# One accumulator and hand-on matmuls in both expert stages, and an up product with the tokens stationary

## What is computed

```python
x = x + 0.5 * ffn(layernorm(x));  x = x + attention(layernorm(x));  x = x + 0.5 * ffn(layernorm(x))

# ffn: E = 64 experts, each token picks K = 6, an expert takes its first CAP = 128 tokens
scores = softmax(xf @ gate_w.T);  _, idx = top_k(scores + gate_b, K)
h  = silu(einsum("ecd,eid->eci", xb, w1)) * einsum("ecd,eid->eci", xb, w3)   # I = 176 hidden
yb = einsum("eci,edi->ecd", h, w2)
y  = zeros_like(xf).at[tok].add(contrib * weight)    # a token can get rows from several experts
z  = silu(xf @ ws1.T) * (xf @ ws3.T) @ ws2.T         # the shared expert, for all tokens
```

## Time and profile before

| | |
|---|---|
| median of three runs | 2036.9 us (2029.87 to 2038.8) |
| the profiled execution | 2036.17 us, its span 2034.4 us |
| PE busy | 1796.7 us (88%) |
| DVE busy | 1274.6 us (63%) |
| ACT busy | 1071.4 us (53%) |
| POOL busy | 873.6 us (43%) |
| granted PE clock, mean | 0.957 of full |

### The profile page before, as it was taken

How to read it: one execution, slowest core, us unless ns; L and a number is a source line. 1 busy time by engine, 2 the same in 40 slices (tenths; PEclk the granted TensorE clock), 3 DMA queues, 4 the chain that set the end, 5 groups by cost and what they waited for, 6 DMA issues and landing times. The chain is left out here.

```text
span 2034.4 us, 33948 instructions
## 1 busy us (share of the span) xinstructions
PE 1796.7 (88%) x11458; PEld 1157.8 (57%) x11458; DVE 1274.6 (63%) x3131; ACT 1071.4 (53%) x2132; POOL 873.6 (43%) x938
## 2 busy tenths in 40 slices
PE   5999997999926799999999999999699999888886
PEld 2566564888813344445545445454356656678786
DVE  4778786444336577777777777773477878744333
ACT  3777664111114577777777777777377766401110
POOL 1011010688736666556655566640101101146675
PEclk9999999999967899999999999999799999989998
DMA  2435442999843344444444444331232433269886
GB/s 86 132 100 164 133 130 103 245 260 260 208 110 94 104 116 116 116 118 125 125 124 119 132 119 116 95 85 43 77 101 79 134 109 103 75 163 227 224 219 120
DMA packets 218389, 270.03 MB, mean 133 GB/s; under 512 B 18394, under 2 KB 185466, under 8 KB 218238
## 3 DMA queue, kind: packets, MB, share of 16 engines
q1 hardware_dynamic: 193662, 230.33, 37.4%
q0 software_dynamic: 24576, 37.77, 9.9%
HBM read 136.17 MB, written 80.38 MB: 106 GB/s over the span
## 5 line engine op out<-in xcount | busy, mean ns | idle before, releaser
L1340 DVE TENSOR_REDUCE a_smax<-a_p_ring 128x1 f32<-128x512 f32 (+2 forms) x768 | 353.8, 505 | 153.7 <-PE a_p_ring L1427 148.6
L1242 ACT ACTIVATE a_probs<-a_p_ring 128x512 f32<-128x512 f32 x640 | 363.9, 606 | 104.2 <-PE a_p_ring L1439 102.6
L1427 PE MATMUL a_p_ring<-p_ks,p_qs 100*128 100x512 bf16 (+3 forms) x1024 | 247.4, 306 | 46.0 <-ACT a_probs L1242 20.6
L634 ACT ACTIVATE e_silu<-e_p_up 88x256 f32<-88x256 f32 x128 | 48.7, 380 | 424.6 <-PE e_p_up L703 328.9
L47 POOL TENSOR_TENSOR f_rstd<-f_mv,eps 128x4 f32<-128x4 f32 x32 | 25.6, 800 | 557.1 <-DVE f_mv L41 552.6
L703 PE MATMUL e_p_up<-e_xT,h_w 128*88 128x128 f32 x2048 | 255.5, 280 | 0.8 <-DVE e_xT L644 0.8
L1439 PE MATMUL a_p_ring<-p_qs,p_ks 103*128 103x512 bf16 (+3 forms) x1024 | 244.2, 305 | 7.0 <-ACT a_probs L1242 6.7
L703 PEld LDWEIGHTS e_p_up<-e_xT,h_w 128*88 128x88 f32 x2048 | 240.4, 163 | 1.3 <-issue 1.1
L455 PE MATMUL f_p_up<-f_xnT,f_ws1T 128*128 128x512 f32 x384 | 188.0, 612 | 1.5 <-ACT f_xnT L250 1.5
L586 POOL DMA_INDIRECT e_got<-rows,slot_token x128 | 127.3, 995 | 140.5 <-issue 134.0
L496 PE MATMUL f_p_z<-f_ws2T,f_hidden 128*128 128x256 f32 (+1 forms) x768 | 184.6, 391 | 1.9 <-DVE f_hidden L343 1.9
(11 more groups left out here) (154 smaller groups left out, 3297.6 us busy)
## 6 DMA issues: line engine op xcount, KB each, us to landing
h_w<-w_in SPq DMA_DIRECT2D x128, 352.0 KB
p_qs<-a_parts SPq DMA_DIRECT2D x192, 128.0 KB, 2.5
p_ks<-a_parts SPq DMA_DIRECT2D x192, 128.0 KB, 2.5
h_w<-w_in SPq DMA_DIRECT2D x128, 176.0 KB
rows<-f_row SPq DMA_DIRECT2D x32, 640.0 KB, 6.8
h_x<-x_in SPq DMA_DIRECT2D x16, 512.0 KB, 5.9
acc<-h_x SPq DMA_DIRECT2D x16, 512.0 KB, 2.8
acc<-blank SPq DMA_DIRECT2D x16, 512.0 KB, 4.1
```

Source lines behind the costliest of these rows:

```text
L1242: nc.scalar.activation(to[:], p_score[s][:], ACT.Exp, scale=SCALE).then_inc(score_free[s], 1)
L1340: ins = nc.vector.tensor_reduce(smax[:, t, 4 * g + h:4 * g + h + 1], p_score[s][:, at:at + length], AX.X, ALU.max)
L1427: ins = nc.tensor.matmul(p_score[s][:, at:at + length], qs[1 - u][0:SR + MASK, 4 * g + h, t * P:(t + 1) * P], ks[1 - u][0:SR + MASK, 4 * g ...
```

## The change

- Both expert stages take one table. Every expert but the first gets the shared rows of the one before it: `down` of e ends with a join matmul (now for all e > 0), `scale` adds it, and expert e writes its rows shared with e+1 to spare rows. The adds go out one by one, each waiting for that of e-2; two neighbours may be in flight together.
- `find_pairs` ahead of the loop becomes `find_shared(g)` for a group of four experts inside the loop, with PE's part (`spread`, one matmul for each expert) there too.
- `up` has the 128 tokens stationary and the weights moving: 2 matmuls of 352 columns in place of 8 of 128. The hidden layer then lies with tokens on partitions, so PE transposes it (`turn_hidden`, 2 transposes) and ACT copies it back (`bring_hidden`). `down` of an expert comes one turn of the loop later. `p_turn` has one buffer, not two.
- The `odd` table goes: its zeroing, its load, the sum, the store back and the waits on them.
- The set-up of the attention on DVE is cut into five pieces, done after experts 12, 16, 20, 24 and 28; the masks are placed by SP after its last weight load.
- The loops of the expert stages are written out in full on all engines.
- At the program's start two more dummy stores are issued (seven, not five).

```diff
@@ route_and_share, SP
                     sp.dma_start(acc[c], x[u][:]).then_inc(acc_stored[u], 16)
-                    if odd is not None:
-                        sp.dma_start(odd[c], w.blank[:, 0:D].unsqueeze(1).to_broadcast([P, NT, D])
-                                     ).then_inc(odd_zeroed, 16)
...
                 loop(sp, chunk)
-                if odd is not None:
-                    sp.wait_ge(odd_zeroed, 16 * N)
@@ experts, POOL
-                if in_pairs:
-                    pool.wait_ge(redirected, 1)
-                for e in range(0, E if in_pairs else 0, 2):
-                    pool.wait_ge(y_scaled, e + 2)
-                    wait_count(pool, added[0], 16 * e)
-                    add(e, e % LANES)
-                    add(e + 1, (e + 1) % LANES)
...
-                    for n in range(e + LANES, min(e + LANES + 2, E)):
-                        gather(n, n % LANES)
...
+                for e in range(E):
                     pool.wait_ge(y_scaled, e + 1)
                     if e + LANES < E:
-                        gather(e + LANES, e % LANES)
-                    wait_count(pool, added[e % len(accs)], 16 * (e // len(accs)))
-                    add(e, e % LANES)
...
+                        gather(e + LANES)
+                    wait_count(pool, added[e % 2], 16 * (e // 2))
+                    if e % GROUP == 0:
+                        pool.wait_ge(redirected, e // GROUP + 1)
+                    add(e)
@@ experts, PE
-                    for g in range(4):
-                        for h in range(DC):
-                            ins = nc.tensor.matmul(p_up[s % 2][0:IH, g, :], w13[s][:, h, g * IH:(g + 1) * IH],
-                                                   xT[s % 2][:, h, :], start=(h == 0), stop=(h == DC - 1))
+                    for h in range(DC):
+                        ins = nc.tensor.matmul(p_up[e % 2][:, 0:SI], xT[e % 2][:, h, :], w13[e % slots][:, h, :],
+                                               start=(h == 0), stop=(h == DC - 1))
...
+                    wait_count(pe, hiddenT_ready, e)
                     for g in range(2):
...
+                        ins = nc.tensor.transpose(p_hidden[:, g, :], hidden[e % 2][:, g * IH:(g + 1) * IH], w.ident[:])
+                    ins.then_inc(hidden_turned, 1)
...
+                    if e:
                         pe.wait_ge(y_scaled, e)
-                        ins = nc.tensor.matmul(p_join[:], same[:, e // 2, :], y[s - 1][:], start=True, stop=True)
...
+                        if (e - 1) % GROUP == 0:
+                            pe.wait_ge(redirected, (e - 1) // GROUP + 1)
+                        ins = nc.tensor.matmul(p_join[:], same[(e - 1) // GROUP % 2][:, (e - 1) % GROUP, :],
+                                               y[(e - 1) % LANES][:], start=True, stop=True)
...
+                for e in range(E + 1):
+                    if e + 2 < E:
+                        turn(e + 2)
+                    if e + 1 < E:
+                        up(e + 1)
+                    if e < E:
+                        turn_hidden(e)
+                    if e:
+                        down(e - 1)
+                    if e % GROUP == 2 and e // GROUP + 1 < E // GROUP:
+                        spread(e // GROUP + 1)
@@ experts, DVE
+                for e in range(E + 1):
+                    if e + 2 < E:
+                        bring(e + 2)
+                    if e + 1 < E:
+                        multiply(e + 1)
+                    if e:
+                        scale(e - 1)
+                    if e % GROUP == 2 and e // GROUP + 1 < E // GROUP:
+                        find_shared(e // GROUP + 1)
+                    if pre and e % GROUP == 0 and 3 <= e // GROUP < 8:
+                        set_up_attention(nc, dve, w, pre, e // GROUP - 3)
@@ attention
-                    sp.dma_start(x_odd[:], odd[n]).then_inc(x_loaded, 16)
...
-                        elif step[0] == "SUM":
-                            add_odd(j + 1)
...
-                    act.wait_ge(x_stored, 16 * n + 16)
                     act.wait_ge(scales_ready, n + 1)
```

More of the change, by code:

```diff
@@ L30 @@
 LANES = 8
+GROUP = 4
 XR = 4
@@ L676, in find_pairs @@
                     dve.drain()
-                    nc.vector.tensor_tensor(aside[:], aside[:], shared_with[:], ALU.mult)
+                    nc.vector.tensor_reduce(handed_on[g % 2][:, 0:n], same[g % 2][:, 0:n, :], AX.X, ALU.add)
                     dve.drain()
-                    nc.vector.tensor_tensor(slot_to[:], aside[:], token[:, 0:E:2], ALU.add).then_inc(redirected, 1)
-                if pre:
-                    set_up_attention(nc, dve, w, pre)
-                if in_pairs:
-                    find_pairs()
-                    pipeline_written(bring, multiply, scale)
-                else:
-                    pipeline(dve, bring, multiply, scale)
+                    nc.vector.tensor_tensor(moved[g % 2][:, 0:n], aside[:, some], handed_on[g % 2][:, 0:n], ALU.mult)
@@ new lines, in find_shared @@
+                    dve.drain()
+                    nc.vector.tensor_tensor(slot_to[:, some], moved[g % 2][:, 0:n], token[:, some],
+                                            ALU.add).then_inc(redirected, 1)
+                tokens()
+                bring(0)
+                find_shared(0)
+                bring(1)
+                multiply(0)
+                for e in range(E + 1):
[9 more added lines that the diff above has]
+                        set_up_attention(nc, dve, w, pre, e // GROUP - 3)
@@ L1654 @@
     small[:, 2] = 2 * CAP - 1
+    small[:, 3] = DUMMY + 2 * P + lanes
     small[:, 4:] = 1 + np.arange(TOK // P)
```

320 lines of the change are left out of this document (147 added, 173 removed).

## The result

The changed kernel takes 1977.51 us (median of four runs, 1970.14 to 1980.8), the kernel before 2036.16 in the same session: ratio 0.971, 95% interval 0.968 to 0.975. The change is faster by 59 us. The forecast was 1983 us with a range of 1968 to 2010.

A forecast was written before the change was run, and what follows sets the result against it. POOL was taken to pace the first expert stage, the pair wait to slow the second, PE to bound the attention. Terms -42.8, +1.5, -3.8, +1.0, -9 sum to -53.1: 2036.2 becomes 1983 us, 8-in-10 range 1968 to 2010.

The forecast's parts named there:

- Second expert stage, -42.8: Second expert stage: 219.8 us instead of 262.6, with start 17.5 and 55 experts at 3.26 each.
- The bounds 3.23 and 3.35: Second expert stage, steady pace per expert: between POOL's floor of 3.23 us and 3.35; 3.26 was taken.
- PE's turn, 3.17: Expert stages: PE's summed records per expert come to 3.17 us, 0.34 more than before and 0.06 under POOL's 3.23.
- rival 4: Expert stages: weight loads show in the new matmul shapes, PE's turn 5.1 us, time 2213 us; chance 0.01.
- POOL's floor, 3.23: Second expert stage: POOL needs gather 1.00, add 1.63 and two gaps of 0.30, so 3.23 us an expert.
- The chain of y, 1.7 us and cost 0: Expert stages: each y needs the one before; join, scaling and adding take about 1.7 us, under the pace, costing 0.
- First expert stage, +1.5: First expert stage: pace 3.26 costs +3.9, fewer early waits give -3, start and tail +0.6.
- Edge, -3.8: Before the next stage: without SP's zeroing of `odd` and its landing, that stage begins 3.8 us earlier.
- Attention, -9: Attention's ramp: first batch -2.4, PE's wait at 620 -4.3, its wait at 672.13 -2.3; full turns 0.
- rival 5: Second expert stage: the pair wait did not hold it, pace stays 3.75 us, +27, time 2010 us; chance 0.04.
- rival 1: Both expert stages: landing of adds becomes the pace, 3.45 us an expert, +21, time 2004 us; chance 0.20.
- Rival 2: Early waits vanish, adds run at their floor, the attention gains 14 us: time 1971 us; chance 0.09.

The follow-up runs named there:

- changed_again: The changed kernel without any edit, run and traced again: 1973.13 us, ratio 0.968 to the kernel before.
- weights_later: The changed kernel with the attention's weight loads moved from ahead of the first expert stage's weight loads to behind that of expert 24: 1979.61 us, ratio 0.972.
- double_join: The changed kernel with each joining matmul issued twice into the same bank: 2018.56 us, ratio 0.993.
- pair_wait: The changed kernel with POOL sending adds two by two in both expert stages, each pair waiting for the pair before: 2052.34 us, ratio 1.008.
- masks_spread: The changed kernel with the six mask loads moved from behind the last weight load to behind those of experts 33 to 53: 1975.48 us, ratio 0.971.
- old_sum: The changed kernel with the second table put back for the attention (zeroing, load, sum, store back, waits): 1988.55 us, ratio 0.978.
- sum_load: The changed kernel with the attention's second table loaded and summed again, but without the store back and its waits: 1985.48 us, ratio 0.975.
- sum_only: The changed kernel with only POOL's sum put back in the attention, adding a tile of zeros: 1979.5 us, ratio 0.974.
- less_dma: The changed kernel loading one row, not 88, of each w2 from the ninth expert on, 21% fewer bytes: 1970.18 us, ratio 0.966.

## Why the prediction was right

The time was forecast within 6 us (1983 against 1977.5), and the mechanism was the likeliest case. Single terms were off by up to 7 us, and some of these errors cancel: against changed_again (-56.9) the second stage is 2.8, the edge 2.3 and the attention's ramp 3.4 us better than forecast, the first stage 3.2 worse. Term by term, against the profiled execution (whose 1970.1 is 7 below the median of its kernel):

- **Second expert stage, -42.8: measured -45.8.** Steady 55 x 3.27 = 180.1 against 179.3 + 1.0 forecast; from add 55 to the end 21.92 against 21.95. The step that was off is the start: it was taken as 17.5 us from the first stage's 17.16, and was 14.8. That row carried a cost of its own stage, the attention's weights on the DMA engines, as weights_later showed (16.25 to 14.86; the other 0.9 of 17.16 went with the change itself). The bounds 3.23 and 3.35 held the pace.
- **PE's turn, 3.17: measured 3.16** (double_join), and with the old up product 3.49 against 3.50 by the same terms. No weight load shows in the new shapes; rival 4 fell with the first trace. By the Trainium skill's two rules on loads (TensorE: Matmul & The Clock Gate, section LDWEIGHTS for what a load takes, section The mechanism for its overlap only where row groups differ) the turn would have been some 4.8, an estimate; this trace disagrees. The same section also lets a load run ahead into a background weight buffer, and that clause fits the trace. The forecast's "waits for gathers left in it" did not show in the steady part: PE had eight buffers of lead and did not use them up.
- **"So the cheaper up product pays for the rest and wins no time itself".** Right as put: without it the kernel is 30 to 36 us slower, because PE's turn would be 3.5 and the bound. It shows how near the cover was: 0.02 us.
- **POOL's floor, 3.23 by an add of 1.63: it is 3.18.** The 1.63 of the earlier trace rows belongs to the first add of a pair or of a stage (all of pair_wait's take 1.61 to 1.63, and so does the row at 1766.32), not to `slot_to`: the 13 adds here that had waited for longer than the usual gap took 1.59 too. Landings put 0.07 on top, so the pace came out right for a partly wrong reason.
- **The chain of y, 1.7 us and cost 0.** Measured 1.6 (435.55 to 437.17), with the slack of 1.3 us that was forecast; at 2.2 it still cost nothing in the steady part. `find_shared` and DVE's pieces stay hidden too, but for a fill of 1.76 us on DVE at 437.72, behind which PE waited 0.83 us.
- **First expert stage, +1.5: measured +0.5 and +4.7.** The parts were off with opposite signs: the waits before add 55 fell by 4.6 in one trace and not at all in the other (forecast 3), the start by 0.9, and "the masks come back at the end, where DMA is less busy" was wrong. The tail grew by 5.6 us: the masks' transfers held up the landing of expert 54's add, and expert 56's, which needs it, waited 5.18 us. masks_spread takes that away, without a gain in the whole. "Within 3 us of before" holds in one trace and not in the other.
- **Edge, -3.8: measured -4.1, and -6.1 in changed_again; program's start, +1.0: measured +1.0.**
- **Attention, -9: measured -12.4 and -15.6 in the ramp.** This was the mis-sized term. The first batch's -2.4 was -2.8. The -4.3 at 620 was -4.8 in the one trace and -3.4 in the other (second transposes less first). The -2.3 at 672.13 was wrong in kind: that wait went from 5.05 to 4.22 only (4.99 in changed_again), though the stretch up to it is shorter by 2.8 and 1.2. The last 5.1 us, from there to the first output (84.8 before, 79.7 in both traces), were not forecast: 3.0 of them go with the store back (84.7 in old_sum, 81.7 in sum_load) and 1.9 with POOL's sum (81.6 in sum_only). The prediction priced waits alone; the 3.0 come with a granted clock of 0.92 in place of 0.88 and 4.0 us less busy time of PE. In the full turns the term is 0, as taken.
- **Pair wait (rival 5) and the landings (rival 1).** pair_wait rules out the first. The prediction's own sign of rival 1, waits for landings in more than one add of ten, did appear: 13 of 55 adds in both stages, 14 and 16 in changed_again. It was a poor sign, for the waits are short: less_dma leaves landings 4 us in the second stage and 1 to 7 in the first, where rival 1 had 21 in all.
- **DVE's fills.** The Trainium skill (SBUF — State Buffer, section SBUF: two separate sides) says that a VectorE operation in a two-port mode keeps GpSimd from writing descriptors, and names a float32 copy as such an operation. The prediction's 4 us took the fills for such operations, which that section does not say. In the fill's time here, 437.72 to 439.48, falls the gather at 438.68 of 0.99 us, as long as any other: the fill did not hold POOL up.

Rival 2 had 1971, and the profiled execution has 1970.1: in that trace the attention (15.6 gained in the ramp against 14) and the early waits (4.6 less) came as it said, but the adds did not run at their floor. The median lies between it and the forecast.

## What to carry to other kernels

A wait for a whole batch of transfers costs their landing once per batch even where each engine is far from full; chaining each transfer to the one two before it, and handing the shared rows on by a small matmul, hid all but 0.07 us an expert of it in the second stage. Before a part is added to an engine under such a floor, sum its turn record by record: start-to-start times from a stretch without waits gave PE's new turn to 0.01 us, and doubling one small instruction on the chip then reads the true turn off the pace. A start-up figure borrowed from another stage carries that stage's transfers with it, and a step taken out of a ramp can be worth more than its own length (POOL's sum of 2.34 us: 5.3 to 8.5), in part because the matmuls behind it run at a higher granted clock; in the full turns it is worth nothing.

## What the runs showed of the hardware

- An accumulating indirect DMA of 128 rows costs POOL 1.59 us and a gather 0.99, with 0.30 between instructions, whichever table of addresses it uses; in pair_wait 5.1 us pass from the start of a pair's second add to the first of the next (1870.26 to 1875.36). The first add of a pair takes 0.04 us more; a wait alone does not do that.
- 21% fewer bytes lowered the share of the DMA engines by a tenth only (0.99 to 0.89, 262 to 206 GB/s, first stage of less_dma).
- 4 records of 352 moving columns take 1.19 us and 16 of 128 take 1.74, both at a granted clock of 1.00: 1408 and 2048 moving columns, 0.85 ns each, whether 4 or 16 weight loads go with them.
- The issue of a mask load on SP took 0.84, 0.64, 1.19, 4.33, 1.63 and 2.98 us, in this order, where six followed one another (changed kernel, 538.75 to 550.58).
- In the attention's ramp one stretch of the same work ran at a granted clock of 0.88 (old_sum, before) or 0.92 (sum_load, sum_only, changed kernel), and PE was busy 75.2 us or 71.0 to 71.9 in it.
